# Graph kernel, edge stage: message buffers moved from SBUF to PSUM, low parts formed in their own batch, and one filter load moved

## The reference, cut to what matters

```python
hs = xs @ w_in2f_s / sqrt(B)                  # 32 scalars per node
hv = einsum('nbc,bf->nfc', xv, w_in2f_v) / sqrt(B)   # 32 vectors of 3 per node
s, v = hs[idx_j], hv[idx_j]                   # gathered by edge
ys, yv = Yr_ij[:, 0], Yr_ij[:, 1:4]
t_s1 = s * ys[:, None]
t_s2 = einsum('efc,ec->ef', v, yv) * IS3      # dot product of two 3-vectors
t_v1 = s[:, :, None] * yv[:, None, :]
t_v2 = v * ys[:, None, None]
h = ssp(f_ij @ W1 + b1)
Wf = ((h @ W2 + b2) * rcut_ij[:, None]).reshape(-1, F, 6)   # filters
edge = concat([t_s1 * Wf[..., 0], t_s2 * Wf[..., 1], t_v1 * Wf[..., 2], t_v2 * Wf[..., 3], ...])
agg = segment_sum(edge, idx_i, num_segments=n)
```

## Time and profile before

| | |
|---|---|
| median of three runs | 2565.68 us (2557.02 to 2566.22) |
| the profiled execution's own time | 2557.94 us |
| its span in the profile | 2556.1 us |
| mean granted TensorE clock | 0.971 of full speed |
| PE, DVE, ACT, POOL busy, share of the span | 94%, 70%, 36%, 64% |
| last stage, share of the chain that ended last, lines L1612 to L1614 | 73% |
| edge stage, first matmul L1875 to the copy of the sums L1467 | 634.3 to 875.5 us |

### The profile page before, as it was taken

One profiled execution on the slowest core, in us unless ns is written; L12 is line 12 of the kernel. 1 busy time (PEld: TensorE's weight loads), 2 busy tenths in 40 slices (PEclk: granted clock), 3 DMA queues, 4 the chain that ended last, 5 costly groups with the idle time before them and its releaser, 6 DMA issues.

```text
span 2556.1 us, 34212 instructions
## 1 busy us (share of the span) xinstructions
PE 2400.7 (94%) x11520; PEld 2002.0 (78%) x11520; DVE 1779.6 (70%) x2626; ACT 921.0 (36%) x1124; POOL 1641.0 (64%) x721
## 2 busy tenths in 40 slices
PE   6989978888898779999999999999999999999999
PEld 6879776777897667777777777777777777777777
DVE  8983336658886587777777777777777777777775
ACT  3741236523886622222222222222222222222221
POOL 0023423238888747777777777777777777777773
PEclk9998979989998879999999999999999999999999
DMA  3024110023432102122221212121222212121211
GB/s 78 16 66 154 34 67 16 1 76 79 107 93 69 57 33 99 66 98 75 89 92 72 98 66 98 66 98 69 95 85 79 98 66 98 66 98 66 98 66 37
DMA packets 49887, 190.87 MB, mean 75 GB/s; under 512 B 13300, under 2 KB 17911, under 8 KB 33444
## 3 DMA queue, kind: packets, MB, share of 16 engines
q1 hardware_dynamic: 35728, 177.90, 19.9%
q0 software_dynamic: 13200, 10.75, 2.0%
q10 hardware_dynamic: 900, 1.44, 0.2%
HBM read 177.54 MB, written 12.35 MB: 74 GB/s over the span
## 4 chain that ended last, share of the span: by engine, by line
PE 82%; DVE 9%; POOL 4%; issue 2%; ACT 1%; DMA 1%; SPq 0%; DVEq 0%; ACTq 0%; POOLq 0%
PE PS L1612 25%; PE PS L1614 24%; PE PS L1613 24%; POOL gatW L741 2%; PE PS L1875 2%; PE PS L1690 2%; PE PS L1876 2%; DVE hotS L1103 1%; DVE hotD L1104 1%; DVE negmax L1321 1%; POOL XN L741 1%; DMA fil<-filters 1%; DVE XTl L1076 0%; DVE XN L1067 0%; PE PS L1754 0%
## 5 line engine op out<-in xcount | busy, mean ns | idle before, releaser
L1562 DVE SCALAR_TENSOR_TENSOR XN<-PS,attn,XN 125x512 f32<-125x512 f32 x1083 | 805.7, 749 | 441.2 <-PE PS L1614 432.5
L771 POOL TENSOR_TENSOR OPl<-TS,OPh 128x1024 fp32r<-128x1024 f32 x256 | 676.7, 2644 | 117.4 <-ACT OPh L1013 117.4
L771 POOL TENSOR_TENSOR OPl<-RAW,OPh 128x1024 fp32r<-128x1024 f32 x192 | 554.8, 2889 | 275.0 <-ACT OPh L1013 274.9
L1612 PE MATMUL PS<-OPh,XTh 128*125 128x512 f32 x1280 | 507.3, 396 | 2.0 <-DVE attn L1516 2.0
L1614 PE MATMUL PS<-OPh,XTl 128*125 128x512 f32 x1280 | 505.9, 395 | 0.0
L1613 PE MATMUL PS<-OPl,XTh 128*125 128x512 f32 x1280 | 503.5, 393 | 0.0
L1013 ACT ACTIVATE OPh<-TS 128x1024 fp32r<-128x1024 f32 x256 | 271.8, 1062 | 529.0 <-PE PS L1614 519.1
L1013 ACT ACTIVATE OPh<-RAW 128x1024 fp32r<-128x1024 f32 x192 | 203.9, 1062 | 581.3 <-PE PS L1614 581.3
L1612 PE MATMUL PS<-OPh,Sh 128*125 128x512 f32 x1024 | 404.8, 395 | 3.7 <-DVE XN L1559 3.7
L1614 PE MATMUL PS<-OPh,Sl 128*125 128x512 f32 x1024 | 404.1, 395 | 0.0
L1613 PE MATMUL PS<-OPl,Sh 128*125 128x512 f32 x1024 | 402.6, 393 | 0.0
(11 more groups left out here) (314 smaller groups left out, 3352.2 us busy)
## 6 DMA issues: line engine op xcount, KB each, us to landing
RAW<-in_values SPq DMA_DIRECT2D x64, 2048.0 KB, 7.5
filters<-filt SPq DMA_DIRECT2D x14, 672.0 KB
fil<-filters SPq DMA_DIRECT2D x11, 840.0 KB
Wraw<-in_ffn SPq DMA_DIRECT2D x4, 1024.0 KB, 5.6
Wraw<-in_L_q SPq DMA_DIRECT2D x2, 1024.0 KB, 5.0
Wraw<-in_L_k SPq DMA_DIRECT2D x2, 1024.0 KB, 7.5
Wraw<-in_L_v SPq DMA_DIRECT2D x2, 1024.0 KB, 7.0
gatW<-nodes,dstI POOLq DMA_INDIRECT x90, 3.6
```

Source lines behind the costliest of these rows:

```text
L771: g.tensor_tensor(OPl[:, j], operand_source(j, parity), OPh[:, j].bitcast(F32), ALU.subtract).then_inc(op_lower, 1)
L1562: v.scalar_tensor_tensor(out=XN[:, t], in0=PS[0:P, bank, :], scalar=w, in1=XN[:, t], op0=ALU.mult, op1=ALU.add).then_inc(v_added, 1)
L1612: mm(dst, lh, rh, start=start, stop=False, skip_group_check=resumed)
```

## The change

1. `vy`, `dot` and `msg` are no longer buffers in SBUF. `vy` lies in PSUM bank 4, `msg` in banks 5 to 7, one buffer of each. A filler keeps the other SBUF buffers at their addresses.
2. The dot product is one `tensor_reduce` over the three parts of `vy`, written to `msg` row 1, in place of two adds; L1451 then multiplies that row by filter 1 in place. There are six steps in a batch (EDGE_STEPS = 6).
3. `lower` works on the batch itself, after its one-hot rows, and no longer on the batch before. The next batch's first product waits until it has ended (`msg_lower`), since `vy` and `msg` have one buffer.
4. `proj2` uses PSUM slots 0, 1, 0. Unit 0 is added to X ahead of the first batch's messages, units 1 and 2 after its low parts.
5. SP asks for the filters of chunk 1 right behind those of chunk 0, ahead of the value matrices.

```diff
-EDGE_STEPS = 7
+EDGE_STEPS = 6
...
+for m in range(len(TILES)):
+    SLOT[("proj2", m)] = m % 2
...
-            vy = sb("vy", [P, 2, EB, 3, F], F32, s)
-            dot = sb("dot", [P, 2, EB, F], F32, s)
-            msg = sb("msg", [P, 2, EB, 9, F], F32, s)
+            sb("below_msgh", [P, 2, EB, 13, F], F32, s)
...
+        vy = PS[0:P, 4, 0:EB * 3 * F].rearrange("p (t c f) -> p t c f", c=3, f=F)
+        msg = PS[0:P, 5:8].rearrange("p b n -> p (b n)")[:, 0:EB * 9 * F].rearrange("p (t k f) -> p t k f", k=9, f=F)
...
             fil_load(0, 0)
+            fil_load(1, 1)
...
             v_load(0, 0)
 
-            for c in range(1, NCH):
-                if c >= 2:
-                    sp.wait_ge(edge_step, EDGE_STEPS * NB * (c - 1))
+            for c in range(2, NCH):
+                sp.wait_ge(edge_step, EDGE_STEPS * NB * (c - 1))
                 fil_load(c, c % 2)
...
-                    a.activation(msgh[:, q].rearrange("p t (k f) -> p t k f", f=F), msg[:, q, :, 0:8, :], ACT.Copy).then_inc(msg_upper, 1)
+                    a.activation(msgh[:, q].rearrange("p t (k f) -> p t k f", f=F), msg[:, :, 0:8, :], ACT.Copy).then_inc(msg_upper, 1)
...
-            def add_projection():
-                for m, tiles in enumerate(TILES):
+            def add_projection(units):
+                for m in units:
+                    tiles = TILES[m]
...
+            add_projection((0,))
             for c in range(NCH):
...
-                    if not before(n, 2):
-                        dve.wait_ge(msg_lower, n - 1)
-
-
-                    v.tensor_tensor(vy[:, q], node[:, :, 1:4, :], y, ALU.mult).then_inc(edge_step, 1)
-                    v.tensor_tensor(msg[:, q, :, 0:9:8, :], fil_[:, :, 0:4:2, :], node[:, :, 0:1, :].to_broadcast([P, EB, 2, F]),
+                    if not before(n, 1):
+                        dve.wait_ge(msg_lower, n)
+
+                    v.tensor_tensor(vy, node[:, :, 1:4, :], y, ALU.mult).then_inc(edge_step, 1)
+                    v.tensor_tensor(msg[:, :, 0:9:8, :], fil_[:, :, 0:4:2, :], node[:, :, 0:1, :].to_broadcast([P, EB, 2, F]),
                                     ALU.mult).then_inc(edge_step, 1)
                     after(1)
-                    v.tensor_tensor(dot[:, q], vy[:, q, :, 0, :], vy[:, q, :, 1, :], ALU.add).then_inc(edge_step, 1)
-                    v.tensor_tensor(msg[:, q, :, 3:8:2, :], fil_[:, :, 3:4, :].to_broadcast([P, EB, 3, F]), node[:, :, 1:4, :], ALU.mult).then_inc(edge_step, 1)
+                    v.tensor_reduce(msg[:, :, 1, :], vy.rearrange("p t c f -> p t f c"), AX.X, ALU.add).then_inc(edge_step, 1)
+                    v.tensor_tensor(msg[:, :, 3:8:2, :], fil_[:, :, 3:4, :].to_broadcast([P, EB, 3, F]), node[:, :, 1:4, :], ALU.mult).then_inc(edge_step, 1)
+                    after(2)
+                    v.tensor_tensor(msg[:, :, 2:8:2, :], msg[:, :, 8:9, :].to_broadcast([P, EB, 3, F]), y, ALU.mult).then_inc(edge_step, 1)
                     after(3)
-                    v.tensor_tensor(dot[:, q], dot[:, q], vy[:, q, :, 2, :], ALU.add).then_inc(edge_step, 1)
-                    v.tensor_tensor(msg[:, q, :, 2:8:2, :], msg[:, q, :, 8:9, :].to_broadcast([P, EB, 3, F]), y, ALU.mult).then_inc(edge_step, 1)
-                    after(5)
-                    v.tensor_tensor(msg[:, q, :, 1, :], dot[:, q], fil_[:, :, 1, :], ALU.mult).then_inc(edge_step, 1)
-                    if not before(n, 2):
-                        lower(n - 1, 1 - q)
+                    v.tensor_tensor(msg[:, :, 1, :], msg[:, :, 1, :], fil_[:, :, 1, :], ALU.mult).then_inc(edge_step, 1)
                     if not before(n, 2):
                         dve.wait_ge(scattered, n - 1)
                     for u in range(HOT_V):
                         ins = v.tensor_scalar(hotE[:, q, u, :], iota16[:], srcF[:, bass.ds(t0 + u, 1)], None, ALU.is_equal)
                     ins.then_inc(hot_v, 1)
+                    lower(n, q)
                     if before(n, 1):
-                        lower(0, 0)
-                        add_projection()
-            lower(NB * NCH - 1, 0)
+                        add_projection((1, 2))
```

More of the change, by code:

```diff
@@ L1416, in lower @@
                 dve.wait_ge(msg_upper, n + 1)
-                v.tensor_tensor(msgl[:, q].rearrange("p t (k f) -> p t k f", f=F), msg[:, q, :, 0:8, :],
+                v.tensor_tensor(msgl[:, q].rearrange("p t (k f) -> p t k f", f=F), msg[:, :, 0:8, :],
                                 msgh[:, q].rearrange("p t (k f) -> p t k f", f=F).bitcast(F32), ALU.subtract).then_inc(msg_lower, 1)
+            add_projection((0,))
             for c in range(NCH):
```

## The result

The changed kernel takes 2524.32 us (median of four runs, 2520.38 to 2526.19) against 2565.95 (2557.02 to 2573.13) for the kernel before on the same chip: a ratio of 0.984, 95% interval 0.982 to 0.986. The profiled execution took 2526.19 us, its span is 2524.4.

The account below looks back on a forecast made before the run. POOL's gather pace was taken as the bound: gathers ending 28 us earlier and a tail 1.7 shorter gave -29.6 us, 2557.94 to 2528.3, stated as 2530; forecast 2522 to 2537 (0.62), full range 2514 to 2556.

Parts of the forecast that it names:

- rival A: Edge stage: gathers keep their pace, not held by the second SBUF input; only the tail moves, 2556 us; chance 0.08.
- (1): Messages and vy in PSUM: excess per gather falls to 0.12 us, 14 in place of 41.9, gathers end 28 us earlier.
- The mean over random starts: Average wait of a gather beginning at a random time under two-SBUF-input DVE instructions: 0.28 us before, 0.07 after.
- (2): Low parts in the same batch: DVE's loop through ACT becomes 5.85 us, just under the 5.88 of a batch.
- Second bound with no slack: DVE's loop of 5.85 us a batch, against 5.88, becomes a second bound in the edge stage.
- the step that named the gathers as the end of the stage: Gathers, the last starting near 828, plus a 17.9 us tail end the edge stage at 845.9.
- rival D: Gathers find almost no two-input op at their start, end 42 us earlier; PE's 832.4 becomes the end: 2515; chance 0.09.
- rival B: DVE becomes the bound, from a loop of 6.33 us; 2545 at 6.9, 2560 at 7.4; chance 0.17.
- (3): PSUM as output of DVE instructions: taken at nothing; upper bound a loop of 7.4 us, errata-table estimate 6.3.
- (4): Start: proj2 unit 0 begins 1.6 us late, batch 0 at 636.4; PE ends at 832.4, costed at nothing.
- (5): Chunk 1's filters ahead: removes DVE's wait of 5.74 us before 649.08, worth nothing at the end.
- (6): Tail from the last gather's start to the copy of the sums: 17.9 us instead of 19.64, 1.7 less.

Follow-up runs that it names:

- Runs 7: The changed kernel with only the vector products (vy) put back in SBUF, msg left in PSUM: 2527.06 us, ratio 0.9866 to the kernel before.
- run 8: The changed kernel with only the messages (msg) put back in SBUF, vy left in PSUM: 2555.00 us, ratio 0.9974 to the kernel before.
- run 2: The changed kernel with both vy and msg put back in SBUF, one buffer each, all else kept: 2558.22 us, ratio 0.9973 to the kernel before.
- run 5: The changed kernel with the multiply of L1452 (one PSUM, one SBUF input) done twice in every batch: 2537.38 us, ratio 0.9908 to the kernel before.
- the repeat: The changed kernel run again, unedited: 2525.57 us, ratio 0.9846 to the kernel before.
- run 11: The kernel before, with only chunk 1's filters loaded ahead of the values: 2564.95 us, ratio 1.0017 to the kernel before.
- run 3: The changed kernel with chunk 1's filters asked for behind the value matrices again: 2524.81 us, ratio 0.9839 to the kernel before.
- run 9: The changed kernel with the second load of values (2 MB) held back until the last batch's first product: 2523.81 us, ratio 0.9853 to the kernel before.
- run 10: The changed kernel with batch 0's products ahead of the first add, proj2's other PSUM slots and the second values load held back: 2520.47 us, ratio 0.9846.
- run 12: The kernel before, with only the second load of values held back until the last batch's first products: 2556.32 us, ratio 0.9982 to the kernel before.

## Why the prediction was right

The prediction had the cause right and the size of the gain nearly, and the bound of the changed kernel wrong.

**The cause was right**, and it is shown, not only argued: two SBUF inputs of a DVE instruction under a gather's start. Runs 7 and 8 separate inputs from outputs, run 2 gives the size. The second statement of the Trainium skill's page "SBUF — State Buffer" (Who interferes with whom), which stood beside rival A, is contradicted by the 33 us of run 2; its first, that two SBUF inputs contend with GpSimd's reads, agrees.

(1) The gathers: 0.12 us of excess each was forecast, 0.05 came, 6.5 us in place of 14 over the last 119. Those intervals are 35.4 us shorter, for 28 forecast; the first 45, at which the forecast took no gain, bring another 1.9. The mean over random starts was the term that was off most: at 0.07 each it made 8.3 us, but only 12 of the 119 begin under an instruction with two SBUF inputs, for 2.3 us in all. The one-hot rows cost 3.7 us, for 6 forecast. The rows fall in patterns, and in the changed kernel most gathers begin where nothing holds them, while in run 8 the worst case comes again and again. So the last gather starts 259.75 us after the first, not 269.2.

(2) The loop: 5.85 forecast, 5.94 measured. L1421 to the next L1445 is 1.62 us (664.40 to 666.02), where 1.50 was taken. "Second bound with no slack" was right in kind. Because the gathers came out 9.5 us faster than forecast, it is the *first* bound, and the step that named the gathers as the end of the stage is the one that failed: the batches came 5.94 us apart by the loop, with the node rows ready up to 20.9 us ahead, and in run 5 an added 0.57 us came through whole. It is rival D's mechanism with rival B's bound, and B's condition of a loop of 6.33 us held only as long as the gathers ended at 828.

(3) PSUM as output: nothing taken, a hundredth found (0.66 for 0.65); the sum takes 0.66, as priced. The errata table of the Trainium skill's page "VectorE: DVE Perf Modes", from which a loop of 6.3 was estimated, is not what these rows show.

(4) The start and PE's end at 832.4. The copy came at 843.99, 11.6 later. Of that 4.6 is the stages ahead (DVE's last split ends at 625.54, not 620.94). 2.0 is the start itself: proj2's first nine matmuls run at a granted clock of 0.50, TensorE's 1.2 GHz, 0.43 us apart, the later ones at 1.00 and 0.23 apart. PE had been busy 4.59 of the 9.60 us ahead. So unit 0 is ready 7.7 us after the split and not 5.7, which was priced from the mean of all sixty matmuls. 4.6 is the batches 2 to 32: 30 times 0.055 from the loop, 1.2 in one long period from 728.40 to 735.53 that the repeat does not have (ACT and DVE both waited there for PE's L1876; why is open), and 1.8 in the last batches, of which 1.1 is the wait behind the load of values. The last 0.35 is the tail. The windows around proj2's start in the changed kernel, with the granted clock in the third column from the right (0.50 is 1.2 GHz, 1.00 is 2.4), and four of its matmuls:

```profile
616.00:625.60 9.60, 4.59 (x33) 3.67 (x32) 8.01 (x21) 2.36 (x4) 7.77 (x7) 0.85 0.80 160
625.60:629.20 3.60, 3.60 (x9) 2.80 (x10) 0.10 (x1) 0.00 (x0) 2.99 (x3) 0.50 0.19 48
629.60:643.00 13.40, 11.98 (x52) 9.23 (x50) 9.34 (x14) 5.49 (x7) 10.83 (x9) 1.00 0.21 47
```

```profile
626.19 0.63 PE L1613 MATMUL PS<-Wl,XTh 128*125 128x512 f32 x1
626.61 0.63 PE L1614 MATMUL PS<-Wh,XTl 128*125 128x512 f32 x1
...
630.01 0.39 PE L1614 MATMUL PS<-Wh,XTl 128*125 128x512 f32 x1
630.24 0.40 PE L1612 MATMUL PS<-Wh,XTh 128*125 128x512 f32 x1
```

(5) The filters, worth nothing at the end: right on the kernel before, where gathers were the bound (run 11). With the loop as bound it is worth 1 to 2 us (run 3), the price of having named the other bound.

(6) The tail: from the last gather's start to the copy 17.9 was forecast, 22.2 came, since the last gather was no longer what the last batch waited for. With the values late it was 18.1 (run 9) and 18.0 (run 10): the sum of its terms was right for the case it described.

So stage 281.96 against 287.1 forecast. The total landed nearer than its steps did, and that is luck: two of them failed in opposite ways, gathers 9.5 us too slow, and 4.3 us of tail too short.

## What to carry to other kernels

Where GpSimd issues gathers back to back, look at what VectorE is reading when each one begins; one operand moved from SBUF to PSUM can be worth more than an instruction removed. Two periodic rows of work lock into step, so take the excess from the rows as they fall, not from a mean over random starts. When one bound is lowered past the next, price the next one's loop to the hundredth of a microsecond, since thirty batches multiply it; and look at which large load is asked for just when the last small ones are due.

## What the runs showed of the hardware

A GpSimd gather of 125 rows takes 1.21 us and 0.30 to the next; where it starts under a two-SBUF-input instruction of VectorE it is longer by what is left of that instruction less about 0.13 us (1.14 for 1.26 left, 0.39 for 0.53). VectorE's sum along a strided row took 0.72 us from SBUF and 0.66 from PSUM, for 480 elements. A load of 2 MB on another queue delayed the rows of a gather already issued by some 6.7 us (820.78, where the 3.26 us from start to landing of the earlier trace rows would give 814.05). In the changed kernel the same load, with a gather from 814.20, came to 5.7 us (823.19 for 817.46).

Six gathers of 4.4 to 4.7 us stand in the traces of the kernel before and its variants: at 654.98 and 849.36 before, at 646.24, 653.01 and 854.88 in run 11, at 654.40 in run 12. One of them, and the low parts that end the row of DVE instructions beside it:

```profile
654.98 4.65 POOL L741 DMA_INDIRECT gatW<-nodes,dstI  x1 [0.30 <-issue]
...
657.07 1.48 DVE L1417 TENSOR_TENSOR msgl<-msg,msgh 125x1280 fp32r<-125x1280 f32 x1
```

The gather starts late in L1442. From there to the end of L1417, at 658.55, DVE runs six more instructions with two SBUF inputs without a gap, and 1.21 + 3.57 - 0.13 is 4.65. The same sum fits each of the others. So these gathers were held through the whole row, not through one instruction. Why only some are is open: at 849.74 in run 11 and at 771.48 in run 12 a gather starts in the same place and takes 1.42 and 1.40 us. Kernels whose low parts wait for the same batch's upper parts have none.
